# Moving the row sums to GpSimd and the sign packing to VectorE in a two-layer convolution kernel, with shorter part rings and a longer image ring

## The chip, the cores and the metric

The kernel runs on one core of one Trainium2 chip, in float32 in and out, with float16 operands for TensorE. The metric is the time of one execution on the device, in microseconds (us), lower is better.

## The reference

The input x is 8 images of 64 channels and 256 x 256 pixels. Two layers follow one another, each on a group-normalised copy of its input, each added back to its input.

```
gn(v): 32 groups of 2 channels, (v - mean) / sqrt(var + 1e-5)      # per image
layer 0:  x = x + G @ P @ A @ depthwise3x3(gn(x))                  # A, G softmaxed 64x64, P 64x64
layer 1:  x = x + conv3x3(sign(gn(x)), sign(w) * mean|w|)          # 64 -> 64 channels
```

Layer 0 is a 3x3 convolution whose nine 64x64 weights are folded ahead of time. Layer 1 needs the sign of the normalised x only, so its products are whole numbers.

## The kernel before

**Tiling.** Even rows of an image lie on partitions 0 to 63 and odd rows on 64 to 127 (64 channels each). A chunk is 4 row pairs (8 image rows, 4 KB for each partition); an image has 32 chunks, the batch 256 (`ALL`). The float32 image stays in `ring`, a ring of 40 chunks in which both layers' results are added in place and from which the output is stored.

**Layer 0.** `normalise` (VectorE, L985) writes one normalised chunk in float32, `xc`, which has a single buffer. `high_part` (ScalarE, L443) rounds it to float16 as `xn`; `low_part` (GpSimd, L355) writes the remainder `xc - xn` as `xl`; `swap_high` (SyncE, L281) copies `xn` by DMA to the other half of the partitions, as `xh`. `xh` and `xl` are rings of 17 rows, four chunks deep; a chunk whose last row is stored a second time at the ring's head (one in four) takes four swap DMAs, any other two. `sums_high` (VectorE, L998) adds `xn` and `xh` to `sh`, from which TensorE gets the products that two rows share. All products go to the PSUM banks `psA`, and `add_layer0` (VectorE, L1005) adds them to the ring.

**Layer 1.** `signs` (ScalarE, L461) writes the signs `sg` of one chunk. Two values are packed into one float16: ScalarE (L469) writes the right half of each row times 1536 to `pk`, and `pack` on GpSimd (L364) adds the left half. TensorE multiplies `pk` into `psB`. `round_b` (ScalarE, L486) rounds to recover the right sums in `rnd`; `add_left` (VectorE) recovers the left ones (L1021) into the other 16 bits of `rnd` and adds them to the ring (L1025); `add_right` (L1030) adds the right ones. `take_part` (VectorE, L813 and L826) takes statistics of a chunk of the next image.

**Order.** Each engine runs its own loop over t = 0 to 255, in program order, with semaphores between them. Step t of TensorE has 31 places k. At its start it waits for the swapped chunk t and for `a_post`; at k = 3 it closes the sums of chunk t-1 (L653, which `add_layer0` waits for), at k = 7 it needs `xl` of chunk t, at k = 13 to 18 `pk` of chunk t-3, and at k = 19 to 21 `sh` of chunk t (L633, which gives `sums_done`). Step t of VectorE is, in this order: `sums_high(t)`, `add_layer0(t-1)`, `add_left(t-4)`, `take_part(t+34)`, `add_right(t-4)`, `normalise(t+2)`. Step t of GpSimd is `low_part(t+1)`, `pack(t-2)`. Step t of SyncE is `swap_high(t+1)`, `load_chunk(t+35)`, which waits for the store of the chunk whose ring place it takes (chunk t-5), then `store_chunk(t-4)`, which waits for `add_right(t-4)`. At steps 29 to 31 of an image VectorE and TensorE also work out the statistics of the next one, with a small matmul into `psL`.

Of the kernel before, what the change touches and what calls it, by code (L numbers as in the profile page):

```python
# [18 lines left out]
RING = 40  # L19
LAG = 3  # L20
BEFORE = 34
SLOTS = 17
# [9 lines left out]
class Chunk:  # L32


    def __init__(self, i):
        self.i = i
        self.par = i % 2
        self.q = i % 4
# [5 lines left out]
def conv_preact(nc, x, att, gatt, pwT, dw, w1T, w1n, ident, same_group, members, out):  # L44
# [32 lines left out]
    def kept(ch):  # L77

        if ch.at(0):
            return [(0, 0, 1), (1, 1, G)]  # L80
        return [(G * ch.q + 1, 1, G - 1 if ch.at(NC - 1) else G)]

    def again(ch):

        return [(0, G, 1)] if ch.q == 3 and not ch.at(NC - 1) else []

    def packed(ch):

        return [(G * ch.q + 1, 1, G - 1)] + again(ch) if ch.q == 3 else kept(ch)
# [8 lines left out]
    def swaps(ch):  # L98

        return (([(0, 0, 1)] if ch.at(0) else []) + [(G * ch.q + 1, 1, shared(ch))] + again(ch))  # L100

    def xh_count(n):

        return 32 * sum(len(swaps(Chunk(m % NC))) for m in range(n % 2, n + 1, 2) if m > 0)
# [18 lines left out]
    with ExitStack() as ctx:  # L123
# [20 lines left out]
        pk = sb("pk", [128, SLOTS - 1, HPW], F16)  # L144
# [69 lines left out]
        right_rdy = sem("right_signs_scaled")  # L214
# [38 lines left out]
        def _(sp):  # L253
# [17 lines left out]
            def swap_high(n):  # L271
                ch = Chunk(n % NC)
# [47 lines left out]
        def _(pool):  # L320
# [28 lines left out]
            def low_part(n):  # L349
                ch = Chunk(n % NC)  # L350
# [16 lines left out]
            low_part(0)  # L367
            for t in range(ALL):
                if t + 1 < ALL:
                    low_part(t + 1)  # L370
                if t + 1 >= LAG:
                    pack(t + 1 - LAG)
            for g in range(ALL + 1 - LAG, ALL):
                pack(g)
# [3 lines left out]
        def _(act):  # L378
# [46 lines left out]
            def high_part(n):  # L425
                ch = Chunk(n % NC)
# [19 lines left out]
            def signs(n):  # L446
                img, i = divmod(n, NC)
                ch = Chunk(i)
# [15 lines left out]
                if n >= 3:  # L464

                    act.wait_ge(b_mm, n - 2)
                act.wait_ge(sg_rdy, n + 1)
                for slot, j, rows in packed(ch):
                    ins = nc.scalar.activation(pk[:, slot:slot + rows], sg[:, j:j + rows, HW:PW], ACT.Copy,  # L469
                                               scale=PACK)  # L470
                ins.then_inc(right_rdy, 1)
# [41 lines left out]
        def _(pe):  # L513
# [124 lines left out]
            def add_shared(n, cross):  # L638
                ch = Chunk(n % NC)
# [40 lines left out]
            def crossing_signs(u, j):  # L680
                ch = Chunk(u % NC)
# [11 lines left out]
            def crossing(t, k):  # L693
                ch = Chunk(t % NC)
# [41 lines left out]
            def straight(t, k):  # L736
                ch = Chunk(t % NC)
# [37 lines left out]
            for t in range(ALL):  # L775
# [8 lines left out]
                for k in range(31):  # L784
                    crossing(t, k)
                    straight(t, k)
                    if a == 0 and k == 10:
# [328 lines left out]
```

## Time and profile before

| | us |
|---|---|
| median of 3 runs | 1887.8 (1884.25 to 1889.64) |
| the profiled execution, its time | 1895.4 |
| its span in the trace | 1893.6 |
| TensorE busy in it | 1759.4 (93%) |
| VectorE busy | 1719.7 (91%) |
| ScalarE busy | 1075.5 (57%) |
| GpSimd busy | 938.3 (50%) |

A busy share says how long an engine had an instruction, not whether that instruction made progress. The trace's timeline gives the start and the duration of each instruction, and in brackets the idle time before it and what ended it. An instruction's recorded duration overlaps the next one's by some 0.07 us on VectorE, so the distance from start to start is what it costs there.

### The profile page before, as it was taken

To read this page: it belongs to the slowest core of one execution; us is meant where nothing else is said; L and a number is where in the kernel's file an instruction comes from. 1 tells how busy PE (TensorE), PEld (TensorE's weight loads), DVE (VectorE), ACT (ScalarE), POOL (GpSimd) and SP (SyncE) were. 2 spreads that over 40 slices of the span, in tenths; PEclk is the share of its full clock that TensorE was granted. 3 is DMA by queue.
4 is the path that set the end of the run, shared out by engine and by line. 5 is a ranking of instruction groups with operands and counts; after the bars stand their busy time and mean duration, and the time that the engine had idled before them with its cause. 6 is when DMAs were issued, how large, how long until landed. Compare 5 with 4: busy or idle time off the path is not lost.

```text
span 1893.6 us, 75000 instructions
## 1 busy us (share of the span) xinstructions
PE 1759.4 (93%) x32458; PEld 1133.2 (60%) x32458; DVE 1719.7 (91%) x2524; ACT 1075.5 (57%) x1409; POOL 938.3 (50%) x675
## 2 busy tenths in 40 slices
PE   0599999999899999999999999999999999999997
PEld 0495557765575556654565555655568668596554
DVE  6889999999999999988999999999999999988886
ACT  2266555666555665555555655566555566566664
POOL 1355545555455554554545545445545555455552
PEclk9999999999999999999999999999999999999999
DMA  9656766777676676666666766667776677555544
GB/s 303 175 155 191 197 196 178 194 200 198 168 198 193 192 203 177 183 193 180 192 175 193 199 184 192 181 187 199 198 199 173 195 199 199 149 124 124 123 119 114
DMA packets 329671, 345.05 MB, mean 182 GB/s; under 512 B 26288, under 2 KB 297584, under 8 KB 329344
## 3 DMA queue, kind: packets, MB, share of 16 engines
q1 hardware_dynamic: 320448, 331.15, 64.6%
q10 hardware_dynamic: 8448, 8.39, 1.5%
q8 instruction: 257, 4.21, 0.9%
q0 software_dynamic: 448, 0.73, 0.2%
q14 instruction: 70, 0.57, 0.1%
HBM read 134.95 MB, written 134.22 MB: 142 GB/s over the span
## 4 chain that ended last, share of the span: by engine, by line
PE 38%; DMA 29%; SPq 16%; DVE 11%; issue 3%; ACT 2%; POOL 0%; DVEq 0%; ACTq 0%
PE psA L568 30%; DMA out_y<-ring 22%; SPq L268 7%; PE psB L568 6%; DMA xh<-xn 5%; SPq L292 4%; SPq L281 4%; SPq L298 2%; DVE ring L1030 2%; DVE bnt L813 2%; ACT xn L443 2%; DMA ring<-in_x 2%; DVE xc L985 1%; PE psA L653 1%; DVE ring L1005 1%
## 5 line engine op out<-in xcount | busy, mean ns | idle before, releaser
L568 PE MATMUL psA<-xh,W0h 64*64 64x512 f16 x9216 | 981.9, 378 | 50.6 <-DMA xh<-xn 43.7
L568 PE MATMUL psA<-xl,W0h 64*64 64x512 f16 (+1 forms) x9216 | 950.4, 377 | 0.0
L355 POOL TENSOR_TENSOR xl<-xc,xn 128x1024 f16<-128x1024 f32 (+1 forms) x320 | 592.8, 1862 | 685.9 <-ACT xn L443 674.7
L568 PE MATMUL psA<-xh,W0l 64*64 64x512 f16 (+1 forms) x4704 | 621.7, 375 | 0.0
L568 PEld LDWEIGHTS psA<-xh,W0h 64*64 64x64 f16 x9216 | 490.1, 106 | 219.4 <-DMA xh<-xn 86.5
L568 PEld LDWEIGHTS psA<-xl,W0h 64*64 64x64 f16 x9216 | 496.5, 107 | 194.5 <-issue 1.9
L568 PE MATMUL psB<-pk,W 64*64 64x512 f16 (+2 forms) x4944 | 604.7, 362 | 3.3 <-POOL pk L364 2.4
L461 ACT ACTIVATE sg<-ring,smalls 128x1024 f16<-128x1024 f32 (+2 forms) x269 | 297.6, 1111 | 271.3 <-DVE ring L1005 270.0
L364 POOL TENSOR_TENSOR pk<-pk,sg 128x520 f16<-128x520 f16 (+2 forms) x320 | 337.7, 1064 | 209.2 <-ACT pk L469 208.9
L1005 DVE SCALAR_TENSOR_TENSOR ring<-psA,smalls,ring 128x1024 f32<-128x1024 f32 x256 | 328.2, 1282 | 87.9 <-PE psA L653 86.5
L568 PEld LDWEIGHTS psB<-pk,W 64*64 64x64 f16 x4944 | 310.9, 107 | 119.9 <-POOL pk L364 4.1
L813 DVE BATCH_NORM_STATS2 bnt<-ring 128x6 f32<-128x512 f32 x512 | 325.5, 679 | 41.0 <-DMA ring<-in_x 40.3
L568 PEld LDWEIGHTS psA<-xh,W0l 64*64 64x64 f16 x4704 | 303.1, 107 | 58.9
L443 ACT ACTIVATE xn<-xc 128x1024 f16<-128x1024 f32 (+2 forms) x262 | 270.8, 1036 | 70.5 <-DVE xc L985 34.0
L486 ACT ACTIVATE rnd<-psB,smalls 128x512 f32<-128x512 f32 x256 | 176.2, 688 | 223.6 <-DVE ring L1030 219.7
L1025 DVE SCALAR_TENSOR_TENSOR ring<-rnd,smalls,ring 128x512 f32<-128x512 f16 x256 | 265.3, 1036 | 9.1
L480 ACT ACTIVATE pf<-psL 128x512 f16<-128x512 f32 x256 | 152.4, 595 | 153.2 <-PE psL L633 152.8
L985 DVE TENSOR_SCALAR xc<-ring,smalls 128x1024 f32<-128x1024 f32 (+3 forms) x261 | 234.7, 901 | 1.1 <-POOL xl L355 0.5
L568 PE MATMUL psA<-xn,W0l 64*64 64x512 f16 x1536 | 219.4, 380 | 0.0
L1030 DVE SCALAR_TENSOR_TENSOR ring<-rnd,smalls,ring 128x512 f32<-128x512 int16 x256 | 218.9, 855 | 0.2
L633 PE MATMUL psL<-sh,W0l 64*64 64x512 f16 (+1 forms) x1536 | 215.5, 374 | 0.8 <-DVE sh L998 0.6
L998 DVE TENSOR_TENSOR sh<-xn,xh 128x1032 f16<-128x1032 f16 (+1 forms) x256 | 181.9, 710 | 21.0 <-issue 13.0
(113 smaller groups left out, 871.0 us busy)
## 6 DMA issues: line engine op xcount, KB each, us to landing
out_y<-ring SPq DMA_DIRECT2D x512, 256.0 KB, 3.8
ring<-in_x SPq DMA_DIRECT2D x448, 256.0 KB, 4.0
xh<-xn SPq DMA_DIRECT2D x494, 129.0 KB, 3.0
ring<-in_x SPq DMA_DIRECT2D x16, 512.0 KB, 16.3
ring<-in_x ACTq DMA_DIRECT2D x16, 512.0 KB, 16.0
xh<-xn SPq DMA_DIRECT2D x126, 32.2 KB, 2.7
xh<-xn SPq DMA_DIRECT2D x16, 96.8 KB, 2.2
pk<-in_w1T POOLq DMA_DIRECT2D x2, 144.0 KB, 6.3
```

What stands on the lines that cost most here:

```text
L355: ins = nc.gpsimd.tensor_tensor(xl[:, slot:slot + rows, 1:W + 1], xc[:, j:j + rows], xn[:, k:k + rows, 1:W + 1], ALU.subtract)
L364: ins = nc.gpsimd.tensor_tensor(here, here, sg[:, j:j + rows, 0:HPW], ALU.add)
L443: ins = nc.scalar.activation(xn[:, k:k + rows, 1:W + 1], xc[:, j:j + rows], ACT.Copy)
L461: ins = nc.scalar.activation(sg[:, j:j + rows, 1:W + 1], ring[:, at:at + rows * W], ACT.Sign, bias=nmean1[img % 2][:, 0:1])
L568: mm = pe.matmul(bank[out0:out0 + C, c0:c1], weights[src0:src0 + C, :], src[src0:src0 + C, slot:slot + rows, width[0]:width[0] + width[1]] ...
L633: mm = pe.matmul(psP[C * half:C * half + C, 0:count * W], W0l[k0:k0 + C, dx, 1, :], sh[k0:k0 + C, at:at + step * (count - 1) + 1:step, dx: ...
L813: ins = nc.vector.bn_stats(bnt[:, ds(2 * s + g, 1), :].rearrange("p a s -> p (a s)"), src[:, 512 * g:512 * g + 512])
L985: ins = nc.vector.tensor_scalar(xc[:, j:j + rows], ring[:, at:at + rows * W], mean0[:, 0:1], rstd0[:, 0:1], ALU.subtract, ALU.mult)
L998: nc.vector.tensor_tensor(sh[:, 0:rows], xn[:, k:k + rows], xh[:, lo:lo + rows], ALU.add).then_inc(sh_rdy, 1)
L1005: nc.vector.scalar_tensor_tensor(out=here, in0=psA[:, ch.par, :], scalar=osc[:, 0:1], in1=here, op0=ALU.mult, op1=ALU.add).then_inc(a_post, 1)
L1025: nc.vector.scalar_tensor_tensor(out=here[:, :, 0:HW], in0=left, scalar=wmean[:, 0:1], in1=here[:, :, 0:HW], op0=ALU.mult, op1=ALU.add)
L1030: nc.vector.scalar_tensor_tensor(out=here[:, :, HW:W], in0=right, scalar=wmean[:, 0:1], in1=here[:, :, HW:W], op0=ALU.mult, op1=ALU.add).t ...
```

## The change

- `RING` goes from 40 to 41 chunks. `load_chunk` still loads chunk t+35 at step t, but takes the place of chunk t-6, not t-5.
- `SLOTS` goes from 17 to 13 rows: `xh` and `xl` are three chunks deep. One chunk in three is now stored twice at the head and takes four swap DMAs and a second `low_part` instruction.
- `sums_high(n)` moves from VectorE to GpSimd, behind `low_part(n)`. Each waits for the swap DMAs of chunk n and for `sums_done` of chunk n-1.
- `pack` moves from ScalarE and GpSimd to VectorE, as one instruction with two SBUF inputs (two where the chunk ends the `pk` ring, one in four), between `add_right` and `normalise`. It waits for `signs` of its chunk and for `b_mm`.
- `add_left` keeps the left values in `psL` (PSUM, float32), not in `rnd` (SBUF).
- `mean_average` and `mean_of_x1` move from the first to the second step of an image, and the small matmuls into `psL` wait for `add_right`, since the bank is now used.

```diff
-RING = 40
+RING = 41
-SLOTS = 17
+SLOTS = 13
+PLACES = 16
...
         self.q = n % 4
+        self.z = n % 3
...
+    def again(ch):
+
+        return [(0, G, 1)] if ch.z == 2 and not ch.at(NC - 1) else []
...
-                if RING <= t + RING - LAG - 2 < ALL:
-                    load_chunk(t + RING - LAG - 2)
+                if RING <= t + RING - LAG - 3 < ALL:
+                    load_chunk(t + RING - LAG - 3)
...
-            def pack(n):
-
-                pool.wait_ge(right_rdy, n + 1)
-                for slot, j, rows in packed(Chunk(n % NC)):
-                    here = pk[:, slot:slot + rows]
-                    ins = nc.gpsimd.tensor_tensor(here, here, sg[:, j:j + rows, 0:HPW], ALU.add)
-                ins.then_inc(pk_rdy, 1)
...
+            def sums_high(n):
+                ch = Chunk(n)
+                rows, lo = shared(ch), G * ch.z + 1
+                if n > 0:
+                    pool.wait_ge(xh_in[n % 2], xh_count(n))
+
+                    pool.wait_ge(sums_done, n)
...
+                nc.gpsimd.tensor_tensor(sh[:, 0:rows], xn[:, k:k + rows], xh[:, lo:lo + rows],
+                                        ALU.add).then_inc(sh_rdy, 1)
+
+            for n in range(ALL):
+                low_part(n)
+                sums_high(n)
...
+            def pack(n):
+                if n >= 3:
+
+                    dve.wait_ge(b_mm, n - 2)
+                dve.wait_ge(sg_rdy, n + 1)
+                for slot, j, rows in packed(Chunk(n)):
+                    ins = nc.vector.scalar_tensor_tensor(out=pk[:, slot:slot + rows], in0=sg[:, j:j + rows, HW:PW],
+                                                         scalar=PACK, in1=sg[:, j:j + rows, 0:HPW], op0=ALU.mult,
+                                                         op1=ALU.add)
+                ins.then_inc(pk_rdy, 1)
...
-                return here, rnd[:].bitcast(I16)[:, :, 0:2 * HW:2], rnd[:].bitcast(F16)[:, :, 1:2 * HW:2]
+                return here, rnd[:].bitcast(I16)[:, :, 0:2 * HW:2], psL[:, 0, 0:G * HW].rearrange("p (s w) -> p s w", s=G)
```

The order of VectorE's instructions in one step of the main loop, before (rows name the output, the inputs and the semaphores waited for):

```order
L1005 SCALAR_TENSOR_TENSOR ring<-psA,smalls,ring 128x1024 [waits a_products]
L1021 SCALAR_TENSOR_TENSOR rnd<-rnd,psB 128x512 [waits rounded_ready,y_ready]
L1025 SCALAR_TENSOR_TENSOR ring<-rnd,smalls,ring 128x4x128 [waits suma_ready]
L813 BN_STATS bnt<-ring 128x6 [waits ring_load_odd]
L813 BN_STATS bnt<-ring 128x6
L826 TENSOR_REDUCE colp<-ring 128x2
L1030 SCALAR_TENSOR_TENSOR ring<-rnd,smalls,ring 128x4x128
L985 TENSOR_SCALAR xc<-ring,smalls 128x1024 [waits xlow_ready]
L998 TENSOR_TENSOR sh<-xn,xh 128x1032 [waits shared_products_done,xhigh_swapped_even,xhigh_plain_ready]
```

The same place of the changed kernel:

```order
L1005 SCALAR_TENSOR_TENSOR ring<-psA,smalls,ring 128x1024 [waits a_products]
L1021 SCALAR_TENSOR_TENSOR psL<-rnd,psB 128x512 [waits rounded_ready,y_ready]
L1025 SCALAR_TENSOR_TENSOR ring<-psL,smalls,ring 128x4x128 [waits suma_ready]
L814 BN_STATS bnt<-ring 128x6 [waits ring_load_even]
L814 BN_STATS bnt<-ring 128x6
L827 TENSOR_REDUCE colp<-ring 128x2
L1030 SCALAR_TENSOR_TENSOR ring<-rnd,smalls,ring 128x4x128
L996 SCALAR_TENSOR_TENSOR pk<-sg 128x520 [waits signs_ready,b_products]
L986 TENSOR_SCALAR xc<-ring,smalls 128x1024 [waits xlow_ready]
```

The sum L998 is gone, the packing L996 stands ahead of the normalisation, and L1025 reads one operand from PSUM. On GpSimd the same stretch of the main loop was, before:

```order
L355 TENSOR_TENSOR xl<-xc,xn 128x4x256 [waits xhigh_plain_ready]
L355 TENSOR_TENSOR xl<-xc,xn 128x256
L364 TENSOR_TENSOR pk<-pk,sg 128x520 [waits right_signs_scaled]
L355 TENSOR_TENSOR xl<-xc,xn 128x4x256 [waits xhigh_plain_ready]
L364 TENSOR_TENSOR pk<-pk,sg 128x520 [waits right_signs_scaled]
```

and of the changed kernel:

```order
L360 TENSOR_TENSOR xl<-xc,xn 128x4x256 [waits xhigh_plain_ready]
L360 TENSOR_TENSOR xl<-xc,xn 128x256
L375 TENSOR_TENSOR sh<-xn,xh 128x1032 [waits shared_products_done,xhigh_swapped_even]
L360 TENSOR_TENSOR xl<-xc,xn 128x4x256 [waits xhigh_plain_ready]
L375 TENSOR_TENSOR sh<-xn,xh 128x1032 [waits shared_products_done,xhigh_swapped_odd]
```

A 520-element addition that waited for the signs has given way to a 1032-element one that waits for the swap DMAs.

## Rows read from the trace of the kernel before

**Rows 1.** The page's busy times, and its granted clock in 40 slices.

```profile
PE 1759.4 (93%) x32458; PEld 1133.2 (60%) x32458; DVE 1719.7 (91%) x2524; ACT 1075.5 (57%) x1409; POOL 938.3 (50%) x675
...
PEclk9999999999999999999999999999999999999999
```

**Rows 2.** Timeline of PE: the first matmuls of steps 72 and 73 (start, length).

```profile
584.88 0.82 PE L568 MATMUL psA<-xh,W0h 64*64 64x512 f16 x12
...
591.60 0.82 PE L568 MATMUL psA<-xh,W0h 64*64 64x512 f16 x12
```

**Rows 3.** L1005 by its line (duration ns min/median/max, first and last start).

```profile
L1005 DVE SCALAR_TENSOR_TENSOR ring<-psA,smalls,ring x256: 1270/1284/1286, 81.2 to 1874.1; 128x1024 f32<-128x1024 f32 x128
```

**Rows 4.** The waits of the engines, and of SyncE's queue (us, times, longest).

```profile
PE psA L568 <- DMA xh<-xn: 43.7, 54, 2.6
...
SPq L261 <- DMA out_y<-ring: 265.2, 188, 3.7
```

**Rows 5.** Timeline of VectorE over step 72.

```profile
585.99 1.28 DVE L1005 SCALAR_TENSOR_TENSOR ring<-psA,smalls,ring 128x1024 f32<-128x1024 f32 x1 [0.39 <-PE psA L653]
587.19 0.74 DVE L1021 SCALAR_TENSOR_TENSOR rnd<-rnd,psB 128x512 f16<-128x512 int16 x1
587.96 0.96 DVE L1025 SCALAR_TENSOR_TENSOR ring<-rnd,smalls,ring 128x512 f32<-128x512 f16 x1
588.84 1.27 DVE L813 BATCH_NORM_STATS2 bnt<-ring 128x6 f32<-128x512 f32 x2
590.04 0.15 DVE L826 TENSOR_REDUCE colp<-ring 128x2 f32<-128x8 f32 x1
590.11 0.74 DVE L1030 SCALAR_TENSOR_TENSOR ring<-rnd,smalls,ring 128x512 f32<-128x512 int16 x1
```

**Rows 6.** Timeline of ScalarE and SyncE in the same step.

```profile
585.16 1.06 ACT L443 ACTIVATE xn<-xc 128x1024 f16<-128x1024 f32 x1
...
589.87 0.60 ACT L480 ACTIVATE pf<-psL 128x512 f16<-128x512 f32 x1 [0.58 <-PE psL L633]
...
586.25 1.41 SPq L281 DMA_DIRECT2D xh<-xn  x2
```

**Rows 7.** Timeline of VectorE and GpSimd at 1688 us.

```profile
1687.97 0.74 DVE L1030 SCALAR_TENSOR_TENSOR ring<-rnd,smalls,ring 128x512 f32<-128x512 int16 x1
1688.63 1.66 DVE L985 TENSOR_SCALAR xc<-ring,smalls 128x1024 f32<-128x1024 f32 x1
1690.21 0.69 DVE L998 TENSOR_TENSOR sh<-xn,xh 128x1032 f16<-128x1032 f16 x1
...
1688.38 1.37 POOL L364 TENSOR_TENSOR pk<-pk,sg 128x520 f16<-128x520 f16 x1 [0.88 <-ACT pk L469]
```

**Rows 8.** Single lines of VectorE (ns min/median/max).

```profile
L1025 DVE SCALAR_TENSOR_TENSOR ring<-rnd,smalls,ring x256: 750/972/1970, 102.0 to 1887.8; 128x512 f32<-128x512 f16 x128
...
L1021 DVE SCALAR_TENSOR_TENSOR rnd<-rnd,psB x256: 723/736/753, 101.3 to 1887.0; 128x512 f16<-128x512 int16 x128
...
L985 DVE TENSOR_SCALAR xc<-ring,smalls x261: 401/803/1757, 67.3 to 1857.9; 128x1024 f32<-128x1024 f32 x117, 128x768 f32<-128x768 f32 x7, 128x1280 f32<-128x1280 f32 x4, 128x256 f32<-128x256 f32 x3
...
L998 DVE TENSOR_TENSOR sh<-xn,xh x256: 555/684/2425, 73.0 to 1865.1; 128x1032 f16<-128x1032 f16 x128
```

**Rows 9.** Timeline of GpSimd: `low_part` and one packing, unhindered.

```profile
579.59 2.07 POOL L355 TENSOR_TENSOR xl<-xc,xn 128x1024 f16<-128x1024 f32 x1 [2.57 <-ACT xn L443]
582.54 1.18 POOL L364 TENSOR_TENSOR pk<-pk,sg 128x520 f16<-128x520 f16 x1 [0.88 <-ACT pk L469]
```

**Rows 10.** The page's DMA issues (count, KB each, median us to landing), and the trace's spread.

```profile
xh<-xn SPq DMA_DIRECT2D x494, 129.0 KB, 3.0
...
DMA to landing us min/median/max: 1.8/3.0/5.0
```

**Rows 11.** Groups: the largest of the eight statistics of an image.

```profile
L929 DVE BATCH_NORM_AGGREGATE smalls<-bnt 128x2 f32<-128x384 f32 x8 | 15.1, 1884 | 0.0
```

More of the change, by code:

```diff
@@ L32, with __init__ @@
 class Chunk:
[L35 to L38, printed above, removed]
+    def __init__(self, n):
+        self.i = n % 32
+        self.par = n % 2
+        self.q = n % 4
+        self.z = n % 3
     def at(self, number):
@@ L79, in kept, with packed @@
         if ch.at(0):
-            return [(0, 0, 1), (1, 1, G)]
[L81 to L89, printed above, removed]
+            return [(G * ch.z, 0, 1), (G * ch.z + 1, 1, G)]
+        return [(G * ch.z + 1, 1, G - 1 if ch.at(NC - 1) else G)]
+    def again(ch):
+        return [(0, G, 1)] if ch.z == 2 and not ch.at(NC - 1) else []
+    def packed(ch):
+        if ch.at(0):
+            return [(0, 0, 1), (1, 1, G)]
+        if ch.q < 3:
+            return [(G * ch.q + 1, 1, G)]
+        return [(G * ch.q + 1, 1, G - 1)] + ([] if ch.at(NC - 1) else [(0, G, 1)])
     def shared(ch):
@@ L98, in swaps @@
     def swaps(ch):
-        return (([(0, 0, 1)] if ch.at(0) else []) + [(G * ch.q + 1, 1, shared(ch))] + again(ch))
+        return ([(G * ch.z, 0, 1)] if ch.at(0) else []) + [(G * ch.z + 1, 1, shared(ch))] + again(ch)
     def xh_count(n):
-        return 32 * sum(len(swaps(Chunk(m % NC))) for m in range(n % 2, n + 1, 2) if m > 0)
+        return 32 * sum(len(swaps(Chunk(m))) for m in range(n % 2, n + 1, 2) if m > 0)
     def buf(ch, j):
@@ L357, in low_part @@
                 ins.then_inc(xl_rdy, 1)
-            def pack(n):
-                pool.wait_ge(right_rdy, n + 1)
-                for slot, j, rows in packed(Chunk(n % NC)):
-                    here = pk[:, slot:slot + rows]
-                    ins = nc.gpsimd.tensor_tensor(here, here, sg[:, j:j + rows, 0:HPW], ALU.add)
-                ins.then_inc(pk_rdy, 1)
[L367 to L374, printed above, removed]
+            def sums_high(n):
+                ch = Chunk(n)
+                rows, lo = shared(ch), G * ch.z + 1
+                if n > 0:
+                    pool.wait_ge(xh_in[n % 2], xh_count(n))
+                    pool.wait_ge(sums_done, n)
+                else:
+                    pool.wait_ge(xh_rdy, 1)
+                    pool.wait_ge(xh_first, 1)
+                k = buf(ch, 1)
+                nc.gpsimd.tensor_tensor(sh[:, 0:rows], xn[:, k:k + rows], xh[:, lo:lo + rows],
[3 more added lines that the diff above has]
+                sums_high(n)
         @block.scalar
@@ L463, in signs @@
                 ins.then_inc(sg_rdy, 1)
[L464 to L471, printed above, removed]
             def keep_shared(n):
@@ L693, in crossing @@
             def crossing(t, k):
[L694 removed]
+                ch = Chunk(t)
                 if k < 3:
@@ L786, in _ @@
                     straight(t, k)
-                    if a == 0 and k == 10:
+                    if a == 1 and k == 4:
                         mean_average(img)
@@ L987, in normalise @@
                 ins.then_inc(xc_rdy, 1)
-            def sums_high(n):
-                ch = Chunk(n % NC)
-                rows, lo = shared(ch), G * ch.q + 1
-                if n > 0:
-                    dve.wait_ge(xn_rdy, n + 1)
-                    dve.wait_ge(xh_in[n % 2], xh_count(n))
-                    dve.wait_ge(sums_done, n)
-                k = buf(ch, 1)
-                nc.vector.tensor_tensor(sh[:, 0:rows], xn[:, k:k + rows], xh[:, lo:lo + rows],
-                                        ALU.add).then_inc(sh_rdy, 1)
+            def pack(n):
[7 more added lines that the diff above has]
+                ins.then_inc(pk_rdy, 1)
             def add_layer0(img, ch):
@@ L1063, in _ @@
                     stats_of_group(img + 1)
+                if a == 1:
+                    mean_of_x1(img)
                 if t > LAG:
@@ L1083, in _ @@
             add_layer0(*of(ALL - 1))
+            for g in range(ALL + 1 - LAG, ALL):
+                pack(g)
             for g in range(ALL - LAG - 1, ALL):
```

37 lines of the change are left out of this document (18 added, 19 removed).

## The prediction

> **What bounds the kernel now.** I read the busy table first [rows 1]: TensorE 93%, VectorE 91%, the clock at its upper level throughout. Two engines are near full, so the question is what a step costs on each. The timeline of TensorE gives its own price: 584.88 to 591.60, 6.72 us for a step with no wait [rows 2]. The 255 distances between the first and the last `add_layer0` take 1874.1 - 81.2 = 1792.9 us [rows 3], 7.03 each; at 6.72 they would take 1713.6. So 79 us are lost in the main loop, and 100.7 us lie outside it. The waits say where: TensorE's only large one is for the swapped chunk, 43.7 us in 54 places, and SyncE, which issues the swaps, stands 265.2 us in front of its loads until an old output chunk has been stored [rows 4]. The rest goes mostly at the image ends, where VectorE's statistics (1.88 us for the largest instruction alone [rows 11]) come on top of a full step.
>
> VectorE's step, start to start [rows 5], from L1005: 1.20, 0.77, 0.88, 1.20, 0.07, then L1030 0.66 [rows 7] and, from the recorded 0.80 and 0.68 [rows 8] less the 0.07 overlap, L985 0.72 and L998 0.61. The sum is 6.1, under 6.72, and it idled 0.39 us for TensorE there. But L1025 has a minimum of 0.75 and a median of 0.97, L985 0.80 and 1.76 at worst, L998 0.68 and 2.43; L1021, of the same size as L1025, stays within 0.72 to 0.75 [rows 8]. What holds the first three is in rows 7: GpSimd's packing arrives at 1688.38 while L1030 runs, gets through after it, ends at 1689.75, and L985 takes 1.66 us instead of 0.80. **So VectorE and GpSimd exclude one another where the VectorE instruction reads two SBUF tensors, or is the float32 copy-like L985, and the waiting one goes next.** L1005 and L1021 read one operand from PSUM and are never held: 1.27 to 1.29 in all 256 cases [rows 3]. The price of an exclusion: L985 lost 0.86 for a packing that takes 1.18 unhindered [rows 7, 9], so 0.32 less than GpSimd's duration. The worst L998 gives the same: 2.43 - 0.68 = 1.75 for a `low_part` of 2.07, 0.32 less.
>
> The Trainium skill, SBUF — State Buffer, section "SBUF: two separate sides", says that the shared port pair is an exclusive lock, held for the whole instruction while the loser fully blocks. The exclusion agrees; the trace charges 0.32 us less than the whole. By the page's rule, each block below would cost 2.15 instead of 1.83, and the forecast would rise by about 47 us.
>
> **The change part by part.**
>
> *Image ring of 41.* The load of chunk t+35 waits for the store of t-6, issued one more step (6.72 us) ago. The store wait of 265.2 us goes nearly altogether, and with it what it did to the swaps: at most the 43.7 us of TensorE's wait plus the queueing behind it. It is worth this only in steps that TensorE bounds.
>
> *Left values in PSUM.* L1025 then has one SBUF operand, so it costs what L1021 does, 0.74 recorded, 0.68 to the next start, instead of 0.88 in rows 5: -0.2 us for each step. It has L1005 and L1021 as nearest rows; both read PSUM and neither is ever held. Its bounds are 0.66 (as L1030) and 0.77 (L1021 with its successor's wait).
>
> *Row sums leave VectorE.* -0.61 for each step.
>
> *Packing comes to VectorE.* 520 elements, two SBUF inputs, float16. Nearest rows: L1030 and L1025, 512 elements in 0.73 to 0.75, which gives 0.67 to the next start; at the other end L998, a float16 addition of 1032 elements in 0.68, would give 0.36 for 520. The multiply-add instruction is L1025's, so I take 0.67, plus 0.12 where it is split, a quarter of the time: 0.70. Bounds 0.4 and 0.8. It waits for `signs`, which start when L1005 ends and take 1.15 us, 2 us ahead: no wait.
>
> Sum of VectorE's step: 1.20 + 0.76 + 0.68 + 1.27 + 0.66 + 0.70 + 0.72 = 5.99, 0.7 us under TensorE's 6.72. **Without exclusions TensorE would bound every step.** ScalarE loses its 0.64 us copy; it is 57% busy and gives nothing back.
>
> *Row sums on GpSimd.* From rows 9, 1.18 us for 520 elements; 2.07 for 1024 with a float32 input: 1.8 to 1.9 ns for each element over some 0.2, so 1032 elements take 2.15 us (bounds 2.05 and 2.3). Load on GpSimd: 2.07 + 2.15 + 0.3 = 4.5 us of 6.7. It fits. But 4.2 us of GpSimd and L1030 + L996 + L985 = 2.1 us of VectorE now exclude one another in 6.7 us, so what matters is the moment. Put TensorE's step at 0. `xn` is made at 0.28 to 1.34 (585.16 against 584.88 [rows 2, 6]); `low_part` runs from 1.4 to 3.5, beside L1005, L1021, the new L1025: all free. The swaps are issued at 1.37 and 1.94 and land 3.0 us later [rows 6, 10]: 4.9. `sums_done` comes at 4.97 (589.87 [rows 6]). So the row sum is ready at 5.0. VectorE: L1005 at 1.11 [rows 5], L1030 at 1.11 + 1.20 + 0.76 + 0.68 + 1.27 = 5.0, L996 at 5.7, L985 from 6.4 to 7.1. **The row sum arrives just where VectorE's only three excluded instructions stand back to back.** As in rows 7 it goes in after one of them, and the rest waits 2.15 - 0.32 = 1.83. The step becomes 5.99 + 1.83 = 7.82.
>
> Does it stay so? When VectorE bounds, count from the end of L985: +0.05, +1.06 for `xn`, swaps at +1.14 and +1.7, landing +4.1 to +5.6 (for a DMA of 2.4 to 3.9 us; typical +4.7); L985 of the next round stands at +5.27. Up to there the row sum still goes ahead of L985. So a chunk with two swap DMAs is nearly always held, and gets 7.82. Of a chunk with four, the last is issued some 1.9 us after the first and lands at +6.0 or later, behind L985, beside L1005: not held, 6.72.
>
> *Shorter part rings.* One chunk in three has four DMAs, not one in four. They cost SyncE 1.2 us more each, in a queue with room. Their late landing starts TensorE late, and VectorE then waits for L653. I put 0.1 us on the average step for that, an estimate between 0 and 0.4: its landing (+6.0) trails the others' (+4.7) by 1.3 us, in one step of three, and I count a quarter of that.
>
> *Moved mean, new waits on `psL`.* They wait for an `add_right` a step old; 8 images: nothing.
>
> **The sum.** Average step (2 x 7.82 + 6.72)/3 + 0.1 = 7.55. It holds for the steps with statistics, t below 222; the last 34 have none, VectorE then needs 4.7 + 1.83 = 6.55, and they stay at 6.72 = 228.5 us. 221 x 7.55 = 1669. The seven image ends add VectorE's statistics whole, some 6 us each (1.88 [rows 11] and about twenty small ones of 0.2): 42. Main loop 1939 against 1792.9: +146. Span 1893.6 + 146 = 2040, time 2042; the profiled execution stood 7.6 over the median, so 2034, called **2030**.
>
> **Rivals.**
>
> *GpSimd finds the gap (faster).* If the row sums mostly run beside L1005 to L826, because landings slip past +5.3 in the steady state too, or the packing costs 0.4, TensorE bounds all steps: 255 x 6.72 = 1714, some 25 at the image ends, 100.7 outside, 1.8 less 7.6: 1835. For it: VectorE has 0.7 us of slack, ring 41 takes the store wait away, and landings do range to 5.0 us [rows 10]. Against: the median is 3.0. It decides at half the two-DMA chunks: with a third of all steps held the average is 7.09, 1930; with 0.15 of them held it is no change.
>
> *Every chunk held.* Four-DMA chunks as well: 7.82 throughout, 221 x 7.82 = 1728, plus 42, 228.5, 100.7 and -5.8: 2094, and up to 2110 with the row sum at 2.3.
>
> *It is only the store wait that mattered.* If the exclusion were given to VectorE's instructions in a row, with GpSimd waiting for the end of the run, the step would be TensorE's and the time again 1835. Rows 7 speak against it: GpSimd went in between L1030 and L985, which follow without a gap.
>
> By a rule of the Trainium skill, GPSIMD Engine Reference, "Engine selection", a two-input elementwise operation should stay on VectorE, being about 2x slower on GpSimd. Here it is 2.15 against 0.68, over three times; by 2x (1.37, held 1.05) the step would be 7.04 and the time about 1925.
>
> **How the numbers follow.** Forecast (1930 to 2080): 0.60. Every chunk held: 0.18. Gap found, by either road: 0.15. Few held, near 1888: 0.07, of which 0.03 within 0.3%, 0.02 above and 0.02 below. A measurement of this kernel can tell 0.3% (5.7 us) from no change. Faster 0.17, same 0.03, slower 0.80. The range takes in both slower cases and part of the few held, 1890 to 2110, and leaves out the gap.
>
> **What would show it.** After: L986 with a median near 2.6 us instead of 0.80, in two of three steps, each behind a GpSimd L375 of some 2.15; L996 at 0.74; L1025 at 0.74 with no spread; TensorE waiting over 150 us for xh; SyncE's store wait near zero. Wrong would be: L986 at 0.80 mostly (the gap was found), L996 near 0.4, or L375 well off 2.15.

## The result, and the profile after

| | before | changed |
|---|---|---|
| median, us | 1888.72 (4 runs, 1884.25 to 1900.77) | 2023.17 (4 runs, 2020.46 to 2032.52) |
| ratio to before | | 1.071 (95% interval 1.065 to 1.077) |
| the profiled execution, its time / its span, us | 1895.4 / 1893.6 | 2021.3 / 2019.5 |

The change makes the kernel 7.1% slower, some 134 us. The forecast was 2030.

The page's busy times and clock of the changed kernel, which answer to [rows 1]:

```profile
PE 1793.0 (89%) x32458; PEld 1006.3 (50%) x32458; DVE 1853.4 (92%) x2589; ACT 902.9 (45%) x1090; POOL 1145.9 (57%) x638
...
PEclk9999999999999999999999999999999999999999
```

VectorE was given less to do (5.99 us a step in place of 6.1, by the prediction's sum) and is busy 134 us longer: its busy time includes the time in which an instruction is held. TensorE's share fell from 93% to 89%.

VectorE's lines, one by one (duration ns min/median/max, first and last start), answer to [rows 3, 8]; the last is the row sum, now GpSimd's:

```profile
L1005 DVE SCALAR_TENSOR_TENSOR ring<-psA,smalls,ring x256: 1269/1273/1285, 83.2 to 1999.0; 128x1024 f32<-128x1024 f32 x128
L1021 DVE SCALAR_TENSOR_TENSOR psL<-rnd,psB x256: 676/680/697, 105.3 to 2013.0; 128x512 f32<-128x512 int16 x128
L1025 DVE SCALAR_TENSOR_TENSOR ring<-psL,smalls,ring x256: 749/751/753, 106.0 to 2013.7; 128x512 f32<-128x512 f32 x128
L1030 DVE SCALAR_TENSOR_TENSOR ring<-rnd,smalls,ring x256: 735/743/2282, 107.9 to 2014.4; 128x512 f32<-128x512 int16 x128
L996 DVE SCALAR_TENSOR_TENSOR pk<-sg x320: 280/693/2410, 94.3 to 2003.4; 128x520 f16<-128x520 f16 x96, 128x130 f16<-128x130 f16 x32, 128x390 f16<-128x390 f16 x32
L986 DVE TENSOR_SCALAR xc<-ring,smalls x262: 400/807/2529, 67.2 to 1983.7; 128x1024 f32<-128x1024 f32 x117, 128x768 f32<-128x768 f32 x10, 128x1280 f32<-128x1280 f32 x4
L375 POOL TENSOR_TENSOR sh<-xn,xh x256: 1477/2052/3058, 71.8 to 1990.0; 128x1032 f16<-128x1032 f16 x128
```

The main loop, from the first L1005 to the last, takes 1999.0 - 83.2 = 1915.8 us against 1792.9: +123 of the profiled executions' +126. The three lines that read PSUM (L1005, L1021, L1025) have hardly any spread; the three that don't (L1030, L996, L986) reach 2.28, 2.41 and 2.53 us. Counting in the trace those that took over 1.5 us: 2 of L1030, 61 of L996, 102 of L986. Before it was 4 of L1030, 7 of L1025, 3 of L998 and 24 of L985.

What stands behind a long one is seen in VectorE's timeline over one step (start, duration; idle time in brackets):

```profile
825.54 1.27 DVE L1005 SCALAR_TENSOR_TENSOR ring<-psA,smalls,ring 128x1024 f32<-128x1024 f32 x1
826.74 0.68 DVE L1021 SCALAR_TENSOR_TENSOR psL<-rnd,psB 128x512 f32<-128x512 int16 x1
827.45 0.75 DVE L1025 SCALAR_TENSOR_TENSOR ring<-psL,smalls,ring 128x512 f32<-128x512 f32 x1
828.12 1.28 DVE L814 BATCH_NORM_STATS2 bnt<-ring 128x6 f32<-128x512 f32 x2
829.31 0.15 DVE L827 TENSOR_REDUCE colp<-ring 128x2 f32<-128x8 f32 x1
829.38 0.74 DVE L1030 SCALAR_TENSOR_TENSOR ring<-rnd,smalls,ring 128x512 f32<-128x512 int16 x1
830.04 2.41 DVE L996 SCALAR_TENSOR_TENSOR pk<-sg 128x520 f16<-128x520 f16 x1
832.37 0.80 DVE L986 TENSOR_SCALAR xc<-ring,smalls 128x1024 f32<-128x1024 f32 x1
833.09 1.27 DVE L1005 SCALAR_TENSOR_TENSOR ring<-psA,smalls,ring 128x1024 f32<-128x1024 f32 x1
```

and GpSimd's in the same stretch:

```profile
826.79 2.07 POOL L360 TENSOR_TENSOR xl<-xc,xn 128x1024 f16<-128x1024 f32 x1 [1.72 <-ACT xn L449]
829.75 2.14 POOL L375 TENSOR_TENSOR sh<-xn,xh 128x1032 f16<-128x1032 f16 x1 [0.88 <-DMA xh<-xn]
```

The row sum arrives at 829.75, while L1030 runs. It goes in after it, and L996 takes 2.41 us, not 0.69. The step is 833.09 - 825.54 = 7.55 us. `low_part` ran its 2.07 us beside L1005 to L1025 and held nobody.

The waits (us, times, longest), as [rows 4]; the last is ScalarE's, for the normalised chunk:

```profile
PE psA L569 <- DMA xh<-xn: 125.5, 102, 3.2
PEld psA L569 <- DMA xh<-xn: 186.0, 131, 3.7
...
ACT xn L449 <- DVE xc L986: 419.6, 231, 5.1
```

TensorE now waits for the swapped chunk 125.5 us (43.7 before), and that is not a DMA gone slow (its median time to landing is 2.4 us, 3.0 before [rows 10]): the chunk starts late, since ScalarE waits for L986. The loads' wait for old output, 265.2 us before [rows 4], stands in no row of SyncE's waits any more.

### The profile page after: what moved, and what is told of

It reads as the page before. It is cut to its first block, busy times and chain, and to the rows that moved or that the text cites. A ratio compares the mean times of both kernels' runs of the same rounds, so it can differ in the third digit from the quotient of the medians.

```text
span 2019.5 us, 74763 instructions
## 1 busy us (share of the span) xinstructions
PE 1793.0 (89%) x32458; PEld 1006.3 (50%) x32458; DVE 1853.4 (92%) x2589; ACT 902.9 (45%) x1090; POOL 1145.9 (57%) x638
## 4 chain that ended last, share of the span: by engine, by line
DVE 52%; PE 14%; issue 12%; DMA 11%; SPq 7%; ACT 3%; DVEq 0%; ACTq 0%
PE psA L569 11%; DMA xh<-xn 10%; DVE bnt L814 9%; DVE xc L986 9%; DVE pk L996 8%; DVE ring L1005 7%; DVE ring L1030 6%; DVE psL L1021 5%; SPq L286 5%; DVE ring L1025 5%; ACT xn L449 3%; DMA ring<-in_x 2%; PE psB L569 2%; SPq L303 2%; PE psA L654 1%
## 5 line engine op out<-in xcount | busy, mean ns | idle before, releaser
L569 PE MATMUL psA<-xh,W0h 64*64 64x512 f16 x9216 | 978.1, 381 | 132.4 <-DMA xh<-xn 125.5
L569 PE MATMUL psA<-xl,W0h 64*64 64x512 f16 x9216 | 947.1, 381 | 0.0
L360 POOL TENSOR_TENSOR xl<-xc,xn 128x1024 f16<-128x1024 f32 (+2 forms) x347 | 589.9, 1712 | 397.2 <-ACT xn L449 385.9
L375 POOL TENSOR_TENSOR sh<-xn,xh 128x1032 f16<-128x1032 f16 (+1 forms) x256 | 548.9, 2144 | 400.7 <-DMA xh<-xn 312.1
L569 PEld LDWEIGHTS psA<-xh,W0h 64*64 64x64 f16 x9216 | 438.6, 107 | 318.3 <-DMA xh<-xn 186.0
L569 PEld LDWEIGHTS psA<-xl,W0h 64*64 64x64 f16 x9216 | 455.8, 108 | 272.6 <-issue 17.2
L449 ACT ACTIVATE xn<-xc 128x1024 f16<-128x1024 f32 (+2 forms) x262 | 270.7, 1036 | 437.1 <-DVE xc L986 419.6
L1005 DVE SCALAR_TENSOR_TENSOR ring<-psA,smalls,ring 128x1024 f32<-128x1024 f32 x256 | 326.8, 1277 | 125.9 <-PE psA L654 125.8
L569 PEld LDWEIGHTS psB<-pk,W 64*64 64x64 f16 x4944 | 290.0, 108 | 171.9 <-DVE pk L996 9.1
L986 DVE TENSOR_SCALAR xc<-ring,smalls 128x1024 f32<-128x1024 f32 (+3 forms) x262 | 370.8, 1417 | 1.0 <-POOL xl L360 0.7
L996 DVE SCALAR_TENSOR_TENSOR pk<-sg 128x520 f16<-128x520 f16 (+2 forms) x320 | 291.6, 927 | 2.9 <-ACT sg L467 2.9
L569 PEld LDWEIGHTS psA<-xh,W0l 64*64 64x64 f16 x4704 | 274.4, 109 | 35.6 <-issue 0.2
L1025 DVE SCALAR_TENSOR_TENSOR ring<-psL,smalls,ring 128x512 f32<-128x512 f32 x256 | 192.2, 751 | 9.1
L1030 DVE SCALAR_TENSOR_TENSOR ring<-rnd,smalls,ring 128x512 f32<-128x512 int16 x256 | 198.1, 774 | 0.2
```

The lines of the kernel that those rows point to most:

```text
L360: ins = nc.gpsimd.tensor_tensor(xl[:, slot:slot + rows, 1:W + 1], xc[:, j:j + rows], xn[:, k:k + rows, 1:W + 1], ALU.subtract)
L375: nc.gpsimd.tensor_tensor(sh[:, 0:rows], xn[:, k:k + rows], xh[:, lo:lo + rows], ALU.add).then_inc(sh_rdy, 1)
L449: ins = nc.scalar.activation(xn[:, k:k + rows, 1:W + 1], xc[:, j:j + rows], ACT.Copy)
L569: mm = pe.matmul(bank[out0:out0 + C, c0:c1], weights[src0:src0 + C, :], src[src0:src0 + C, slot:slot + rows, width[0]:width[0] + width[1]] ...
L986: ins = nc.vector.tensor_scalar(xc[:, j:j + rows], ring[:, at:at + rows * W], mean0[:, 0:1], rstd0[:, 0:1], ALU.subtract, ALU.mult)
L996: ins = nc.vector.scalar_tensor_tensor(out=pk[:, slot:slot + rows], in0=sg[:, j:j + rows, HW:PW], scalar=PACK, in1=sg[:, j:j + rows, 0:HPW ...
```

## The experiments

Two theories to begin with. **Theory A**, the prediction's: GpSimd's row sum and VectorE's two-SBUF-input instructions exclude one another, and the sum arrives where these stand together. **Rivals**: the shorter part rings, with their more frequent four-DMA chunks, start TensorE late; or the packing is too much for VectorE. Each experiment is timed beside the kernel before (its median was 1889 to 1895 us in these sets), and ratios are to that. Where two experiments of different sets differ by a few us, their ratios are the better guide.

| experiment | median us | ratio (95% interval) |
|---|---|---|
| one more wait on GpSimd (`ordered`) | 1865.81 | 0.985 (0.981 to 0.989) |
| row sums back on VectorE (`sums_back`) | 1875.10 | 0.990 (0.986 to 0.994) |
| half of the row sum (`half_sums`) | 1900.73 | 1.003 (1.000 to 1.005) |
| packing back on ScalarE and GpSimd (`pack_back`) | 1933.97 | 1.017 (1.013 to 1.021) |
| the old rings in the changed kernel (`old_rings`) | 2014.97 | 1.064 (1.059 to 1.069) |
| before with the new rings (`rings_only`) | 1864.09 | 0.987 (0.984 to 0.990) |
| before with left values in PSUM (`left_only`) | 1884.84 | 0.999 (0.996 to 1.002) |
| both of these (`rings_left`) | 1867.09 | 0.988 (0.985 to 0.991) |
| `ordered` with the old rings | 1892.11 | 0.998 (0.995 to 1.002) |
| `ordered`, statistics later (`late_stats`) | 1872.95 | 0.991 (0.988 to 0.994) |

**The same work at another moment.** Of the changed kernel, GpSimd's row sum of chunk n also waits until the normalisation of chunk n + 1 is done, and so falls beside L1006, which reads PSUM.

```diff
                     pool.wait_ge(sums_done, n)
+                    pool.wait_ge(xc_rdy, min(n + 2, ALL))
```

> The changed kernel with one wait more: on GpSimd the row sum of chunk n also waits until VectorE has normalised chunk n+1 (xc_ready at n+2), so it starts behind L986 and runs beside L1005, L1021 and L1025, which the changed kernel's trace shows unhindered (L1025 0.749 to 0.753 us in all 256 cases). Nothing else is altered. Theory A (exclusion: the row sum falls among L1030, L996 and L986 and blocks the rest of them): L986 at 0.80 us almost everywhere, steps at TensorE's 6.72, time 1835 to 1860, under both kernels. Rival B (VectorE simply has more work than before, or GpSimd is too slow for its load): the wait can only delay the row sums, so 2023 or more. Rival C (the swap DMAs, four in one chunk of three, start TensorE late): 1980 to 2030.

Measured: 1865.81 us, 157 us under the changed kernel, 1.5% under before, and 6 over the range of Theory A. No instruction is left out or made smaller. GpSimd's timeline of one step of this kernel, and VectorE's L1006 (the changed kernel's L1005) beside it:

```profile
904.06 1.91 POOL L376 TENSOR_TENSOR sh<-xn,xh 128x1032 f16<-128x1032 f16 x1 [2.78 <-DVE xc L987]
...
904.68 1.28 DVE L1006 SCALAR_TENSOR_TENSOR ring<-psA,smalls,ring 128x1024 f32<-128x1024 f32 x1 [0.79 <-PE psA L655]
```

The normalisation (L987, the changed kernel's L986) by its line, and the page's busy times:

```profile
L987 DVE TENSOR_SCALAR xc<-ring,smalls x262: 407/808/947, 67.4 to 1826.7; 128x1024 f32<-128x1024 f32 x117, 128x768 f32<-128x768 f32 x10, 128x1280 f32<-128x1280 f32 x4
...
PE 1749.4 (94%) x32458; PEld 1414.9 (76%) x32458; DVE 1585.3 (85%) x2589; ACT 911.1 (49%) x1090; POOL 1071.9 (58%) x638
```

GpSimd stood idle 2.78 us until the normalisation was done, and the step did not grow: the median one takes 6.71 us. The normalisation's maximum fell from 2529 to 947 ns, VectorE is busy 268 us less with the same 2589 instructions, and it now waits for TensorE. The row sum alone takes 1.91 us (1907 ns, the median of its line here); the 2.14 of the changed kernel's timeline would then include its wait for L1030 to end.

**Half the dose.** The row sum of two of four rows, all else as changed. Two rows of each chunk's shared products are then not those of the reference.

```diff
                 k = buf(ch, 1)
+                rows = rows if n == 0 else 2
```

> The changed kernel with the row sum on GpSimd cut to two of the four rows (the other two keep the values of the first chunk, so this part of layer 0 is left out). The instruction shrinks from 1.91 us to about 1.0. Theory A: each exclusion costs VectorE 0.95 us less, of 1.6, so the loop loses about 40% of what it lost: with VectorE's 0.75 us of slack a held step goes from 7.6 to 6.72 or just above, time 1850 to 1900. Rival C (late swaps start TensorE late): the time stays within 1% of 2023. Rival B (VectorE's own work): likewise.

Measured: 1900.73 us, 122 below the changed kernel and just at the upper end of Theory A's range. The row sum and the normalisation by their lines:

```profile
L376 POOL TENSOR_TENSOR sh<-xn,xh x256: 1046/1301/2319, 72.0 to 1865.7; 128x516 f16<-128x516 f16 x127, 128x1032 f16<-128x1032 f16 x1
L987 DVE TENSOR_SCALAR xc<-ring,smalls x262: 401/814/1661, 67.4 to 1859.1; 128x1024 f32<-128x1024 f32 x117, 128x768 f32<-128x768 f32 x10, 128x1280 f32<-128x1280 f32 x4
```

Holds there still are: 115 normalisations and 22 packings took over 1.5 us. But each costs at most 0.85 us (1661 - 814), which is near VectorE's 0.7 us of slack. The median held normalisation lost 0.74 us, and the median held packing 0.86, where the changed kernel's lost 1.59 and 1.71: both times the row sum's own duration (1.05 and 1.91) less 0.3 on the one line and less 0.2 on the other. Half the dose gave back 122 of the 157 us that `ordered` gives, not half. That fits a price paid only for the part of a hold beyond the slack.

**Row sums back on VectorE.** The changed kernel with `sums_high` at the start of VectorE's step, and GpSimd with `low_part` alone; rings, packing and PSUM as changed.

```diff
             for n in range(ALL):
                 low_part(n)
-                sums_high(n)
...
+                sums_high(t)
```

> The changed kernel with the row sums back on VectorE at the start of its step, everything else as changed (packing on VectorE, left values in PSUM, rings 13 and 41, GpSimd does the low part alone). VectorE's step is then about 5.95 + 0.61 = 6.55 us, under TensorE's 6.72, and GpSimd's only instruction, 2.07 us, lies beside L1005 to L1025. Theory A (exclusion by the row sums on GpSimd): 1835 to 1870. Rival B (the packing on VectorE is what is too much): VectorE has 0.6 us more work than in the changed kernel, so 2023 or more. Rival C (swap DMAs of the 13-row rings): 1980 to 2030.

Measured: 1875.10 us, 5 over the range of Theory A. The group of the normalisation (busy us, mean ns, idle before) shows it free:

```profile
L971 DVE TENSOR_SCALAR xc<-ring,smalls 128x1024 f32<-128x1024 f32 x234 | 189.2, 808 | 0.0
```

In the changed kernel the mean of the same 234 is 1463 ns.

**The packing.** The changed kernel with the packing back on ScalarE and GpSimd, between `low_part` and the row sum. VectorE has 0.7 us less to do in each step.

```diff
+                if t + 1 >= LAG:
+                    pack(t + 1 - LAG)
+                if t + 1 < ALL:
+                    sums_high(t + 1)
...
+                    ins = nc.scalar.activation(pk[:, slot:slot + rows], sg[:, j:j + rows, HW:PW], ACT.Copy,
+                                               scale=PACK)
...
-                if t + 1 >= LAG:
-                    pack(t + 1 - LAG)
```

> The changed kernel with the packing back on ScalarE and GpSimd; the row sums stay on GpSimd (its step: low part, packing, row sum), rings and left values as changed. VectorE's step has only L1030 and the normalisation left to exclude, and 0.6 us less work: 5.3 us, slack 1.4 us. Theory A (exclusion by the row sums costs 1.6 us each time it falls on them): 5.3 + 1.6 = 6.9 with the packing on GpSimd adding another 0.9 at times, so still slower than with the sums on VectorE (1867): 1890 to 1960. Rival (the packing on VectorE is a necessary part of the loss): 1855 to 1875, like the rings alone.

Measured: 1933.97 us, still 1.7% slower than before. The normalisation (here L1011) by its group:

```profile
L1011 DVE TENSOR_SCALAR xc<-ring,smalls 128x1024 f32<-128x1024 f32 x234 | 387.3, 1655 | 1.9 <-POOL xl L361 1.9
```

This line is held oftener than in the changed kernel, 156 times for over 1.5 us, now that the packing doesn't stand ahead of it. Beside 141 of these ran the row sum, beside 54 of the 141 GpSimd's packing too, and beside 15 the packing alone: a part of the holds is the packing's. Against `rings_left` below, from which the kernel differs by the row sum's engine alone, it is 67 us longer. With the new rings and `psL` in all four, the two moves give:

| median, us | packing on ScalarE and GpSimd | packing on VectorE |
|---|---|---|
| row sums on VectorE | 1867.09 | 1875.10 |
| row sums on GpSimd | 1933.97 | 2023.17 |

By these medians the packing alone costs 8 us, the row sums alone 67, both together 156. The 8 is not clear of noise: the ratios are 0.988 and 0.990, and their intervals overlap. That the two together cost more than their sum fits a slack that the packing uses up and that would have covered a part of each hold.

**The rings.** The changed kernel with the rings of before:

```diff
-RING = 41
-SLOTS = 13
+RING = 40
+SLOTS = 17
```

> The changed kernel with the rings of before: 17 rows of parts (four swap DMAs in one chunk of four), an image ring of 40 chunks, whose loads wait for the store of chunk t-5. Row sums on GpSimd, packing on VectorE and left values in PSUM as changed. Theory A: the exclusions are the same, time 2000 to 2060. Rival C (the 13-row rings and their extra DMAs): 1900 or less. If the store wait of the 40-chunk ring matters in held steps too, above 2060.

Measured: 2014.97 us. The four-DMA chunks are one in four again, and 8 us at most come of it (the ratios are 1.064 and 1.071, with intervals that overlap). The rival of the part rings falls. SyncE's wait for old output came back in part:

```profile
SPq L266 <- DMA out_y<-ring: 120.3, 107, 3.2
```

The opposite, the kernel before with the new rings alone (`RING` 41, `SLOTS` 13, the load one chunk later in the ring, `z = n % 3`):

```diff
-RING = 40
-SLOTS = 17
+RING = 41
+SLOTS = 13
```

> The kernel before with the rings alone changed: parts 13 rows, image 41 chunks. Row sums on VectorE, packing on ScalarE and GpSimd, left values in SBUF, as before. The store wait of SyncE (265 us before) should go, and with it TensorE's waits for xh in most places. Theory A (my step on the ring: worth at most the 79 us that the loop loses, only where TensorE bounds): 1850 to 1880. Rival (the extra four-piece chunks eat it, or VectorE at 6.5 us a step has no slack to use it): 1885 to 1910.

Measured: 1864.09 us, 1.3% faster than before. TensorE's wait for the swaps:

```profile
PE psA L574 <- DMA xh<-xn: 21.8, 15, 3.2
```

It is halved, and the loads' wait for old output, 265.2 us before [rows 4], stands in no row of SyncE's waits. The same once more, from the other side: `ordered` with the rings of before.

```diff
-RING = 41
-SLOTS = 13
+RING = 40
+SLOTS = 17
```

> The ordered kernel (row sums on GpSimd released by the normalisation, 1866 us) with the rings of before: 17 rows, 40 chunks, and so SyncE's wait for the store of chunk t-5. Theory A (with the exclusions gone, what the longer image ring gives is seen again, about 25 us as between the kernel before and the rings alone): 1882 to 1895, no faster than the kernel before. Rival (the ordering alone makes it faster, rings do nothing): 1860 to 1870.

```profile
SPq L266 <- DMA out_y<-ring: 265.0, 187, 2.8
...
PE psA L570 <- DMA xh<-xn: 34.9, 45, 2.3
```

Measured: 1892.11 us, 26 above `ordered`. So the rings are worth 25 us, in either kernel, as long as TensorE sets the step; where VectorE sets it, they are worth nothing that shows. Both rings changed together in every one of these runs. That the gain is the longer image ring's is argued from the store wait, which it alone bears on, and not shown by a run of its own. With the old rings `ordered` equals the kernel before: the row sums and the packing changed places, and nothing was gained. Nor does `ordered` gain on `rings_only`, 1866 against 1864.

**Left values in PSUM.** The kernel before with L1025's operand in `psL`, and the mean moved as in the change.

```diff
-                return here, rnd[:].bitcast(I16)[:, :, 0:2 * HW:2], rnd[:].bitcast(F16)[:, :, 1:2 * HW:2]
+                return here, rnd[:].bitcast(I16)[:, :, 0:2 * HW:2], psL[:, 0, 0:G * HW].rearrange("p (s w) -> p s w", s=G)
```

> The kernel before with the left values in PSUM alone (and the moved mean that goes with it); rings, sums and packing as before. L1025 loses its exclusion by the low part on GpSimd: 0.75 us instead of 1.04 on average, 0.2 to 0.3 us of each VectorE step. Theory A (the store wait is what holds the kernel before in most steps): little, 1875 to 1890. Rival (VectorE's 6.5 us a step is what holds it): 1850 to 1870.

Measured: 1884.84 us, which can't be told from no change. The instruction did what it should, as the groups show (L1034 is L1025, L1039 is L1030):

```profile
L1034 DVE SCALAR_TENSOR_TENSOR ring<-psL,smalls,ring 128x512 f32<-128x512 f32 x256 | 192.3, 751 | 9.2
...
L1039 DVE SCALAR_TENSOR_TENSOR ring<-rnd,smalls,ring 128x512 f32<-128x512 int16 x256 | 245.2, 958 | 0.2
...
SPq L267 <- DMA out_y<-ring: 263.8, 182, 2.6
```

L1025's mean fell from 1036 to 751 ns, but L1030's rose from 855 to 958: it still reads two SBUF tensors, comes earlier now, and meets GpSimd's packing (145 of L1030 are over 0.85 us with the packing beside them, 91 before). So a third of the gain went back. The rest shows nowhere either: the store wait is as it was, and the median step is TensorE's 6.72 us in both kernels. Rings and left values together, with the row sums on VectorE and the packing as before:

> The changed kernel with row sums back on VectorE and packing back on ScalarE and GpSimd: the rings and the left values in PSUM are what is left of the change. Theory A (only the move of the row sums hurts): 1840 to 1865, under each of the two alone, since both stores and VectorE are relieved. Rival (a packing on GpSimd that meets L1030, L985 or L998 costs as the row sums do): 1880 or more.

Measured: 1867.09 us, no better than the rings alone, and 2 us over the range I had given. I had counted on VectorE's shorter step at the image ends; it brought nothing. L1030's median is 1148 ns in this kernel, against 747 before.

**The image ends.** From L1006 to L1006, 203 of the 255 steps of `ordered` lie within 0.06 us of 6.71; the long ones are steps 29 and 30 of an image, 8.8 and 10.4 us, and some just behind them. There VectorE does the statistics ahead of the normalisation. I tried the reverse order on `ordered`:

```diff
-                    if a == SCALE_STEP and k == 4 and img + 1 < NB:
+                    if a == SCALE_STEP and k == 12 and img + 1 < NB:
...
-                if img + 1 < NB:
-                    if a == AGGR_STEP:
-                        stats_parts(img + 1)
...
+                if a == AGGR_STEP and img + 1 < NB:
+                    stats_parts(img + 1)
```

> The ordered kernel (1866 us) with the image end rearranged: at step 29 VectorE normalises chunk 31 first and works out the statistics behind it, and TensorE's statistics matmul stands at k = 12 of step 30 instead of k = 4. In the ordered kernel each image end loses some 6 us in steps 29 to 31 (8.7, 9.9 and 7.5 us instead of 6.72). If that loss is the wait of TensorE for statistics that stand ahead of the normalisation, it shrinks by 1.5 to 3 us for each of 7 images: 1845 to 1857. If it is VectorE's work as such, no change: 1863 to 1868.

Measured: 1872.95 us, 7 more than `ordered` and outside both ranges: a miss. Its timelines of GpSimd and VectorE at the second image end:

```profile
505.06 1.91 POOL L376 TENSOR_TENSOR sh<-xn,xh 128x1032 f16<-128x1032 f16 x1 [2.72 <-DVE xc L987]
506.92 1.58 POOL L360 TENSOR_TENSOR xl<-xc,xn 128x768 f16<-128x768 f32 x1
...
504.81 1.89 DVE L931 BATCH_NORM_AGGREGATE smalls<-bnt 128x2 f32<-128x384 f32 x1
...
506.73 0.26 DVE L932 TENSOR_SCALAR smalls<-smalls 128x4 f32<-128x4 f32 x1
506.91 1.62 DVE L933 TENSOR_SCALAR smalls<-smalls 128x4 f32<-128x4 f32 x1
```

The same instruction in `ordered`:

```profile
277.90 0.22 DVE L933 TENSOR_SCALAR smalls<-smalls 128x4 f32<-128x4 f32 x1
```

An instruction of four elements takes 1.62 us in place of 0.22, and it takes 1.62 at all seven image ends in the loop. It starts as the row sum ends, GpSimd goes straight on with `low_part`, 506.92 to 508.50, and L933 ends at 508.53. The normalisation releases the row sum, and the statistics behind it read SBUF alone: the new order put them where GpSimd works. Steps 29 to 31 together grew by 1.1 us for each image end, which makes the loop's 7.3 us (1767.0 against 1759.7). A hold of 1.4 us on L933 is large enough for that; that it is the cause no run shows by itself.

## Why the prediction was right, and where it was not

**The mechanism was the one named.** The row sum arrives when L1030, L996 and L986 stand in a row, goes in after one, and VectorE waits. The same instructions with one wait more are 157 us faster.

**The price of a hold was too high.** I had 1.83 us, from a row sum of 2.15 less 0.32. The rule holds, duration less 0.3, but the row sum takes 1.91 us where nothing hinders it. So 1.60, and that is what L986 shows (2.40 against 0.80); L996 shows 1.72 (2.41 against 0.69), 0.2 under the duration. The 2.15 was read from a line through two points of different types (a `low_part` with a float32 input), and rounded up: the line itself gives 1.18 + 512 x 0.00177 = 2.08. The float16 addition is cheaper for each element. A slip beside it: every chunk held with the row sum at 2.3 makes a step of 7.97 and a time of 2127, not 2110. The Trainium skill, SBUF — State Buffer, section "SBUF: two separate sides", has the pair held for the whole instruction and the loser blocked; by that a hold would cost 1.91. The trace charges 1.60 to 1.72.

**Who is held was wrong, and the sum right by luck.** All two-DMA chunks should have been held and no four-DMA chunk. Counted over t = 4 to 221 it is 114 of 143 for the two-DMA chunks, and 31 of 73 for the four-DMA ones; the two chunks with more are free. That is 145 of 218, 0.67, just what I had, from two errors that cancel. The swaps landed sooner than [rows 10]; the page's DMA issues of the changed kernel:

```profile
xh<-xn SPq DMA_DIRECT2D x494, 129.0 KB, 2.4
```

With 2.4 us in place of 3.0 a four-DMA chunk can be early enough to collide. It mostly is from the fourth image on (28 of 43, against 3 of 30 in the first three images); why then and not earlier stays open. The moment does decide: counted from the start of L1005, 141 of the 145 held row sums begin within 5.1 us, and 71 of the 73 free ones later, as a rule when L986 has begun or is through.

**The average step** is 7.43 us against the predicted 7.55 (image ends left out): 12 hundredths for 221 steps, 26 us of main loop. By the measured hold and share the sum would have been 0.67 x (5.99 + 1.60) + 0.33 x 6.72 = 7.30. The trace says where the 0.13 above it is. A step with a hold takes 7.52 us on average, and VectorE idles 0.04 us in it. A step without one takes 7.23, not 6.72: VectorE idles 1.33 us in it, and TensorE waits 1.20 us for the swapped chunk. So the term for late landings, 0.1 on the average step, was too small: a free step pays 0.5 us, in three of ten steps. How much of this the clock's drops, below, make up stays open. Held steps 0.3 us shorter than forecast and free steps 0.5 us longer cancel in part: that the forecast came within 7 us is partly luck, too.

**Image ends.** I had 6 us each above the average step; steps 29 to 31 together take 27.8 us on average, 5.5 above 3 x 7.43. Outside the loop it was 103.7 us, not 100.7. The last 32 steps, behind the last image end, take 6.88 each, where I had 6.72.

**The parts.** L1025: predicted 0.74 without spread, measured 0.749 to 0.753. L996: I took 0.74 and it is 0.69, near the row I chose and not the float16 addition's 0.36. SyncE's store wait: near zero was said, and the loads have none. TensorE's wait for the swaps: over 150 us was said, 125.5 is there (186.0 at its weight loads). L375 was to take some 2.15 and has a median of 2.05, with its waits in it. L986's median was to be 2.6; it is 0.81, and this sign failed outright. Had I gone by it alone, "the gap was found" would have been the reading. Holds are spread over two lines, 102 on L986 and 61 on L996, and in neither are they half of the cases. The number to ask for was the count of long ones on all lines, or the step.

**The rivals.** "GpSimd finds the gap" was priced at 1835 and did not happen by itself; when it is made to happen the time is 1866. Most of the difference is in the main loop, for which I had 25 us above TensorE's steps and which has 48: it is 1842.6 - 83.0 = 1759.6 us (L1006's first and last start) against 255 x 6.71 = 1711. Steps 29 to 31 of the images are 36 of these, and the steps just behind them most of the rest. "Only the store wait mattered" is half true: the rings are the one part of the change that gains. The page's rule that GpSimd is about 2x slower for such an operation (the Trainium skill, GPSIMD Engine Reference, "Engine selection") is short of what the trace has, 1.91 us against 0.68, 2.8x. Its advice to keep such operations on VectorE came out: `sums_back` is 148 us faster than the changed kernel, though `ordered` shows the same move to cost nothing when its moment is chosen.

## What to carry to other kernels

Two engines that exclude one another are scheduled by their moments, not by their busy shares: before moving a two-input SBUF operation to GpSimd, find VectorE instructions that read PSUM and make it wait for them: the wait was on an engine with slack, and here gave back 157 us. It did not make the move a gain, for VectorE was not what bounded the step. Read the spread of each line (median against maximum) before its mean, and in a change of several parts look for the one that gains: the rings alone gave all that any version had.

## What the runs showed of the hardware

**TensorE's clock falls after short idle times in a busy kernel.** The changed kernel's windows (stretch, length, busy times of PE, PEld, DVE, ACT and POOL with their counts, granted clock, DMA share, GB/s) around one landing at 267.4 us, and TensorE's timeline there:

```profile
264.00:267.00 3.00, 1.02 (x20) 0.34 (x12) 2.77 (x7) 0.88 (x2) 0.75 (x2) 1.00 0.29 62
268.00:271.30 3.30, 3.30 (x36) 1.45 (x32) 2.20 (x3) 0.92 (x1) 3.30 (x2) 0.50 1.06 304
...
267.45 1.14 PE L569 MATMUL psA<-xh,W0h 64*64 64x512 f16 x12 [2.43 <-DMA xh<-xn]
```

TensorE worked 1.02 us of the first window, at full clock. After 2.43 us without work the clock is 0.50, the 1.2 GHz level, and 36 matmuls take 3.30 us, where an unhindered step does 127 (32458 / 256) in 6.72, 36 in 1.9. The main loop has 16 such drops in the changed kernel, 3 before and 3 in `ordered`, 15 in `old_rings`. Of the 16, 13 last 3.4 us and 3 last 6.8; at 1.4 us for each 3.4 they are at most 27 us of the 157, less where VectorE sets the step anyway. As there are few where the holds are gone, they are a result of the holds more than a rival to them. Not every such idle time brings one: the clock stayed at its upper level behind the 2.51 us at 200.1 us. The page's clock row of 40 slices shows none of it.

**A hold does not ask how large the waiting instruction is.** Four float32 elements waited 1.4 us for GpSimd (L933 above). Just ahead of it a statistics instruction of 384 float32 elements from SBUF (L931, 504.81 to 506.70 us) ran its usual 1.89 us beside the row sum, and neither held the other.

**The place and form of a result count.** L1021 takes 0.68 us when it writes float32 to PSUM, and took 0.74 when it wrote every second float16 of an SBUF tensor [rows 8]. Place, type and spacing changed together, and no run parts them.
